# Two transfers in place of one for each stack of q and k in a hybrid model block

## The reference

```
src: (8, 64, 128) of the function's own set-up; here B, T, d = 16, 256, 128
q = (src @ Wq + bq).reshape(B, T, 16, 8)
k = (src @ Wk + bk).reshape(B, T, 16, 8)
v = (src @ Wv + bv).reshape(B, T, 16, 8)
scores = einsum('bqhd,bkhd->bhqk', q, k) * 8 ** -0.5
probs = softmax(scores)
out = einsum('bhqk,bkhd->bqhd', probs, v).reshape(B, T, d) @ Wo + bo
```

## Time and profile before

| | us |
|---|---|
| median of 3 runs | 2142.91 |
| lowest and highest run | 2138.33, 2144.39 |
| span of the profiled execution | 2142.3 |
| TensorE busy in it | 1930.0 |
| VectorE busy | 1737.5 |
| ScalarE busy | 1487.9 |
| GpSimd busy | 776.3 |

### The profile page before, as it was taken

The page is one execution under the profiler, slowest core; times in us unless marked ns, Lnnn a source line. Parts: engine busy times, 40 slices in busy tenths (PEclk is TensorE's granted clock), DMA queues, the critical chain, the costliest instruction groups (busy, mean ns, idle before and its releaser), DMA issues.

```text
span 2142.3 us, 48053 instructions
## 1 busy us (share of the span) xinstructions
PE 1930.0 (90%) x16928; PEld 1496.9 (70%) x16928; DVE 1737.5 (81%) x4463; ACT 1487.9 (69%) x3207; POOL 776.3 (36%) x1139
## 2 busy tenths in 40 slices
PE   4769899999999999999999999999999999987757
PEld 3556667787777777786777778686777778674535
DVE  5766978989898988989897998989898998764643
ACT  4556758778686868778685868778686877754322
POOL 5313343524244343425244342434244352422120
PEclk9889999999999999999999999999999999997867
DMA  5121222211222222111222222121222221112010
GB/s 159 14 59 12 59 66 59 58 40 47 52 58 66 61 66 61 56 34 55 53 58 66 61 63 60 48 42 49 63 58 66 61 63 52 54 50 73 5 55 6
DMA packets 220734, 117.11 MB, mean 55 GB/s; under 512 B 120520, under 2 KB 206672, under 8 KB 215376
## 3 DMA queue, kind: packets, MB, share of 16 engines
q1 hardware_dynamic: 220496, 114.04, 20.6%
HBM read 67.60 MB, written 46.14 MB: 53 GB/s over the span
## 4 chain that ended last, share of the span: by engine, by line
PE 55%; DVE 18%; DMA 11%; POOL 5%; ACT 4%; issue 3%; SPq 3%; DVEq 0%; POOLq 0%; ACTq 0%
DMA q_max<-qk_scr 8%; DVE nmax L1293 6%; PE psB L722 6%; PE psA L860 5%; PE psB L872 5%; DVE work L1218 4%; PE psA L872 4%; PE psA L697 4%; PE psB L801 3%; PE psB L860 3%; PE psA L628 3%; DMA qk_scr<-kparts 2%; SPq L533 2%; DVE hid L1406 1%; PE psA L708 1%
## 5 line engine op out<-in xcount | busy, mean ns | idle before, releaser
L1245 DVE TENSOR_TENSOR att<-att,QK 128x1024 f32<-128x1024 f32 x192 | 250.3, 1337 | 14.8 <-ACT att L1001 14.7
L1527 POOL TENSOR_TENSOR own<-X,ccoef 128x512 f32<-128x512 f32 x128 | 161.2, 1264 | 213.2 <-PE psA L697 98.2
L1435 POOL TENSOR_SCALAR var_eps<-lnmv 128x2 f32<-128x2 f32 x128 | 40.3, 315 | 539.1 <-DVE lnmv L1108 536.5
L1218 DVE SCALAR_TENSOR_TENSOR work<-psA,c_conv_w,work 128x255 f32<-128x255 f32 (+2 forms) x450 | 195.3, 473 | 11.9 <-ACT work L959 11.8
L1070 ACT ACTIVATE hid<-psA,c_b 128x256 f32<-128x256 f32 x295 | 135.8, 485 | 86.7 <-PE psA L860 86.6
L628 PE MATMUL psA<-xnT_a,c_w_in 128*128 128x256 f32 x608 | 178.6, 398 | 17.6 <-DVE hid L1218 8.2
L1293 DVE TENSOR_REDUCE nmax<-psB 128x2 f32<-128x512 f32 x288 | 186.5, 679 | 1.1 <-PE psB L763 1.0
L860 PE MATMUL psA<-x1T,c_w 128*128 128x256 f32 x608 | 180.3, 396 | 1.3 <-DVE nmax L1293 1.0
L1293 DVE TENSOR_REDUCE nmax<-psA 128x2 f32<-128x512 f32 x224 | 149.7, 680 | 35.7 <-PE psA L763 35.4
L1047 ACT ACTIVATE pt<-psB 128x512 f32<-128x512 f32 x256 | 147.5, 614 | 30.4 <-PE psB L787 30.3
L872 PE MATMUL psB<-c_w,hid 128*128 128x128 f32 x1152 | 161.1, 285 | 0.4 <-ACT hid L1070 0.4
(11 more groups left out here) (326 smaller groups left out, 5384.1 us busy)
## 6 DMA issues: line engine op xcount, KB each, us to landing
qk_scr<-kparts SPq DMA_DIRECT2D x96, 192.0 KB, 2.4
k_stack<-qk_scr SPq DMA_DIRECT2D x32, 576.0 KB
q_stack<-qk_scr SPq DMA_DIRECT2D x32, 576.0 KB
qk_scr<-qparts SPq DMA_DIRECT2D x96, 128.0 KB, 1.9
k_max<-qk_scr SPq DMA_DIRECT2D x32, 256.0 KB
q_max<-qk_scr SPq DMA_DIRECT2D x32, 256.0 KB
lvl_scr<-work SPq DMA_DIRECT2D x32, 192.0 KB, 5.7
qk_scr<-qparts SPq DMA_DIRECT2D x96, 64.0 KB, 2.4
```

Of the source, the lines that this page charges most:

```text
L1218: m = e.scalar_tensor_tensor(out=cv[:, back:], in0=t[:, 0:T - back], scalar=conv_w[:, c, tap:tap + 1], in1=cv[:, back:], op0=ALU.mult, op1 ...
L1245: e.tensor_tensor(att[:, :, :], att[:, :, :], bc(QK[:, kq, :], 1, HG), ALU.mult).then_inc(att_done, 1)
L1527: e.tensor_tensor(own_b[k % 2][:, :].rearrange("p (h c) -> p h c", c=HD), X[:, tt, h0 * HD:(h0 + HG) * HD].rearrange("p (h c) -> p h c", c ...
```

## The change

The fetch of each stack is written as a loop over two ranges of rows, 0 to 63 and 64 to 71. Both transfers add 16 to the stack's semaphore, so the thresholds of those who wait for it go from 16 to 32 a turn: the next store into the scratch on SyncE, and TensorE ahead of `es`. Nothing else differs.

```diff
@@ -535,7 +535,7 @@
                     u = nth[hop]
                     e.wait_ge(split_done[k], u + 1)
                     if u:
-                        e.wait_ge(qk_stacked[k], 16 * u)
+                        e.wait_ge(qk_stacked[k], 32 * u)
@@ -566,8 +566,10 @@
                     for side in (1, 0):
                         e.wait_ge(qk_stored[side], (96, 48)[side] * (u + 1))
-                        e.dma_start((q_stack, k_stack)[side][0:ROW_MAX, :, :].rearrange("r s t -> r (s t)"),
-                                    dram(qk_scrd[side], 0, [[NH * T, ROW_MAX], [1, NH * T]])).then_inc(qk_stacked[side], 16)
+                        for r0, r1 in ((0, 64), (64, ROW_MAX)):
+                            e.dma_start((q_stack, k_stack)[side][r0:r1, :, :].rearrange("r s t -> r (s t)"),
+                                        dram(qk_scrd[side], r0 * NH * T, [[NH * T, r1 - r0], [1, NH * T]])).then_inc(
+                                            qk_stacked[side], 16)
@@ -774,8 +776,8 @@
                     if k == 0:
-                        e.wait_ge(qk_stacked[0], 16 * (nth[hop] + 1))
-                        e.wait_ge(qk_stacked[1], 16 * (nth[hop] + 1))
+                        e.wait_ge(qk_stacked[0], 32 * (nth[hop] + 1))
+                        e.wait_ge(qk_stacked[1], 32 * (nth[hop] + 1))
                         e.wait_ge(max_stacked, 16 * (nth[hop] + 1))
```

## The result

| | before | after |
|---|---|---|
| median, us (4 runs each, same chip) | 2143.65 | 2171.06 |
| lowest and highest | 2138.33, 2144.93 | 2169.37, 2173.07 |
| span of the profiled execution, us | 2142.3 | 2168.5 |

The ratio is 1.0135, with a 95% interval of 1.012 to 1.0149: 27.4 us lost in the medians, 26.2 us in the spans. The forecast was 2144 us with a range of 2134 to 2156 us, so the result lies outside it, on the side of rival A and beyond its price of 2153 to 2159 us.

A forecast was written before the change was run, and what follows sets the result against it. TensorE, busy 90%, was taken to bound the kernel, with q_max's landing able to move the end. To the profiled 2142.3 us, issues, waits and stack landings added 0 and q_max 1: 2143.3, forecast 2144 us, range 2134 to 2156.

The forecast's parts named there:

- rival A: 64 rows on more DMA engines crowd q_max: 0.5 us on 21 to 32 landings, 10 to 16 us slower; chance 0.23.
- What bounds the kernel: TensorE is busy 90%; q_max's landing, 8% of the chain, can move the end, and a stack has 13 us to spare.
- Issues added, and what covers them: 64 more sync-queue issues, 21.3 us (bounds 19 and 31), hidden under waits for q's stores and ScalarE: cost 0.
- Waits changed: Thresholds at lines 538, 777 and 778 go from 16 to 32 a turn; no wait gets a new thing behind it.
- The transfers' own time: The stack's pair lands 0 to 0.5 us earlier (bounds 1.2 earlier, 3.6 later), hidden by 13 us to spare: 0.
- What the stack does to others: k_stack in flight beside q_max shifts its landing: +0.05 us on 21 turns, 1 us; bounds -10 to +11, or +16 us.
- The sign of more engines: Whether spreading the 64 rows over more engines delays q_max or relieves it; the port rule spoke for delay.

The follow-up runs named there:

- 64 + 8: k_stack alone fetched as 64 and 8 rows, against the kernel before: 2175.07 us, ratio 1.0158; the changed kernel divides both stacks so, 2171.06 us.
- 36 + 36: k_stack fetched in two transfers of 36 rows each, q_stack in one of 72, against the kernel before: 2154.34 us, ratio 1.0074.
- 63 + 9: k_stack fetched in two transfers of 63 and 9 rows, q_stack in one of 72, against the kernel before: 2129.29 us, ratio 0.9949.
- 68 + 4: k_stack fetched in two transfers of 68 and 4 rows, q_stack in one of 72, against the kernel before: 2121.95 us, ratio 0.9914.

## Why the prediction was wrong, by its steps

*What bounds the kernel.* This was right: the landing of q_max is what can move the end, not that of a stack; the share of the chain went where it said a loss would show.

*Issues added, and what covers them.* The cover was right, the price was not: an issue took 0.48 to 0.49 us each, so 64 x 0.48 + 64 x 0.49 = 62 us of the queue against 21.3 us before, 41 us more where 21.3 us was taken, above the upper bound of 31 us. Dividing q alone, and both with q first, showed that it costs 0.

*Waits changed.* This was right: nothing waits at line 538, and line 788 waits for no stack. The sync queue's wait for ScalarE ahead of maxT shrank by (447.7 - 431.6) / 32 = 0.50 us a turn, where 0.3 was said, and the one wait for high is 3.4 us in place of 2.6. But the wait for q's stores was to shrink by 0.36 us a turn and grew by 0.46 us, (198.3 - 183.6) / 32. The prediction left out that these stores land behind q_max.

*The transfers' own time.* It was right that this is hidden: k_stack was issued 5.5 us later with the order turned round, and the kernel was faster. The sign was wrong. The pair was to land 0 to 0.5 us earlier; after its first issue k_stack lands at 9.6 us in place of 7.9, and q_stack at 5.8 in place of 5.0. Both lie within the bound of 3.6 us later.

*What the stack does to others.* Here the prediction failed, in two steps. The term was named as the only one that could move the end, and then set to +0.05 us a landing with no row behind that value, and the case of a crowded q_max, rival A, was given a chance of 0.23. The term measured 9.30 - 8.48 = 0.82 us by the pieces of the chain and 0.91 us over all turns. The bound of 0.5 us was taken from the spread of q_max in the kernel before, 8.00 to 9.04 us, where every turn has the same k_stack beside it; a spread among equal neighbours does not bound what another neighbour does. The second step is the count. 21 turns stood in the chain. In 22 turns of the kernel before TensorE's first matmul on q_max starts 0.04 us after the landing, and in the other ten 0.24 to 2.06 us after it, nine of them by at most 0.70 us: there TensorE came a little late, and 0.9 us more of transfer uses that up. In the changed kernel 31 turns start 0.04 us after the landing, and 31 stand in the chain. 21 x 0.82 is 17 us and 31 x 0.82 is 25 us, against 26.2 us measured in the span. The forecast counted 21; the upper end of rival A counted 32, but at 0.5 us each. Rival A was the right one, with its mechanism, its place and its side; 16 us, its upper end, was too little.

The sign of more engines was weighed with a rule on the ports (the Trainium skill, SBUF — State Buffer, "Door 1: The DMA port swizzle"), which spoke for A. The runs agree with what it would do: no division landed k_stack sooner than the 7.9 us of the whole (64 + 8 took 9.6 us), and with both in flight the rate is 165 in place of 190 GB/s. They don't show that it is the ports; the sides of HBM and of the on-chip memory were not tried apart.

*What stays open.* It is open why 36 + 36 crowds q_max more than 72 does, and where the engines meet.

## What to carry to other kernels

Before spreading a transfer over more engines, look for what is in flight beside it: its own landing may have 13 us to spare while its neighbour's has none. Price such a neighbour by a run that takes it away (here, the order of two issues), not by the spread of times with it there, and count the turns that are nearly critical as well. And when a critical transfer is slow for its bytes, divide that one: here this alone gave 35 us, where the division of its neighbour lost 27. Of the 35 us, 19 also came from the order of the two stacks alone, so they are in part the same gain.

## What the runs showed that was not expected

- The row count alone, with the same bytes in the same place, moved the kernel by 2.1%: 63 + 9 rows gave a ratio of 0.9949, 64 + 8 rows 1.0158.
- The sync queue's issue of a part of a stack took 0.48 to 0.49 us (median) where that of the whole took 0.31 to 0.36 us.
- The undivided k_stack had been costing the kernel before 0.9% by its place in the queue.
- Some divisions of k_stack made the kernel faster than one transfer did, as 68 + 4 did by 0.9%, because a stack on fewer engines left q_max alone.
